# A layer-norm chain laid more densely beside the attention stage, and one weight wait placed later

## The chip, the cores and the metric

The kernel runs on one Trainium2 chip (trn2), on 8 cores at once. Each core works on its own 4,096 of the 32,768 tokens; the cores exchange nothing. The metric is the device time of the slowest core, in microseconds.

## The reference

One "macaron" layer on x of 16 x 2048 tokens with 1024 features, in float32:

```python
x = x + 0.5 * ffn(layernorm(x), gate_w, expert_w)
x = x + attn(layernorm(x), Wq, bq, Wk, bk, Wv, bv, Wo, bo)
x = x + 0.5 * ffn(layernorm(x), gate_w, expert_w)

def attn(x, ...):               # 16 heads of 64 features, no product between tokens
    q = exp(-0.5 * (x @ Wq + bq) ** 2)
    k = exp(-0.5 * (x @ Wk + bk) ** 2)
    v = x @ Wv + bv
    coeff = sum(q * k, over the 64 features of a head)
    return (coeff * v) @ Wo + bo

def ffn(x, gate_w, expert_w):   # 8 experts of 1024 x 1024, the best two weighted by a softmax
    w = softmax(top2(x @ gate_w.T)), put back into 8 columns, 0 elsewhere
    return sum over e of w[:, e] * (x @ expert_w[e].T)
```

The layer norm has no scale or bias. Attention has no product between tokens, so every stage works on a tile of tokens alone.

## The kernel before, in words

Each core holds its tokens as 16 tiles of 256, feature-major: a tile is 8 blocks (c) of 128 features x 256 tokens. The expert weights stay in SBUF in bf16 (16 MB, loaded at the start). The attention weights don't fit beside them. They are cast once into a DRAM copy in bf16 and come back in each attention stage as 16 blocks of 512 KB (four of each matrix, 256 output features each), through four buffers (`Wab`). A block's load is issued by SyncE when the last matmul on the block four places earlier is done (`load_for`, L477).

Tiles go in pairs, eight pairs, a on stream A and b on stream B. A stream owns half of the PSUM banks and its scratch tiles (`SA`, `SC`, `yec`, with the stream's letter behind). For each pair the program has six stages (L677 to L684): experts a, experts b, attention a, attention b, experts a, experts b.

Each engine has one queue of instructions, in the order in which the Python program emits them. `run(heavy, chain, delay, stride)` (L632) sets that order: `heavy` is the generator of a stage, which stops (`yield`) after each group of matmuls; `chain` prepares the other tile's next stage and is advanced by one stop at group `delay` and at each `stride`-th after it. What is left of the chain when the stage ends is emitted at once, without matmuls between.

`attn_phase` (L458) has 25 groups. Groups 1 to 8: for each block of 128 output features (dj) 8 query matmuls into one bank (L504) and 8 key matmuls into another (L514). ACT squares the query bank with its bias (L524) and takes exp (L528), VectorE adds the key bias (L533) and squares (L536), ACT takes exp (L539), VectorE multiplies (L543). Both banks are used again by the next dj. Group 9: 8 matmuls sum over the heads (L553, the coefficient). Groups 10 to 17: value matmuls (L572), one matmul that spreads the coefficient (L587), bias and product on VectorE (L592, L596). Groups 18 to 25: out projection (L612), each evacuated by VectorE, which adds it to x (L622); two banks alternate, so a group waits for the evacuation of the group two before it.

`ln_chain` (L196) has 12 stops: (1) two casts of x to bf16 on VectorE (L211, L214); (2) 8 column-sum matmuls (L224); (3) the first two squares on ACT (L244); (4) to (7) two sum-of-squares matmuls each (L252) and the next square; (8) the statistics, five short operations on VectorE (L267 to L274); (9) Ln, Exp and a copy on ACT (L277 to L281); (10) two broadcast matmuls (L285, L286); (11) two copies on ACT (L289, L291) and the first two of four pairs of normalising operations on VectorE (L299, L302); (12) the other two pairs. Attention b begins when all four are done.

In an expert stage GpSimd scales the tile by the gate's weight for each expert (L426) and TensorE multiplies (L436).

Of the kernel before, what the change touches and what calls it, by code (L numbers as in the profile page):

```python
# [25 lines left out]
def build_program(nt_count=NT):  # L26
# [78 lines left out]
    def op(eng, fn):  # L105
        Q[eng].append(fn)

    def wait(eng, s, val):
        if val and val > 0:
            Q[eng].append(lambda e, _s=sems[s], _v=val: e.wait_ge(_s, _v))  # L110

    def inc(eng, fn, s, by=1):
        C[s] += by
        Q[eng].append(lambda e, _f=fn, _s=sems[s], _b=by: _f(e).then_inc(_s, _b))
        return C[s]

    def drain(eng):
        Q[eng].append(lambda e: e.drain())  # L118

    def wait_tok(eng, tok):  # L120
        if tok:
            wait(eng, tok[0], tok[1])
# [31 lines left out]
    for i in range(16):  # L154
        m, j2 = i // 4, i % 4
# [27 lines left out]
    blk_loaded = {}  # L183
# [274 lines left out]
    def attn_phase(St, t):  # L458
# [6 lines left out]
        def lhs(i, c, dj):  # L465
            buf = i % NWB
            base = buf * 2048 + c * 256 + (dj % 2) * 128
            return Wab[:, base:base + 128]
# [8 lines left out]
        def load_for(idx):  # L477
            if idx >= 16:
                return
            b = order[idx]  # L480
            if idx - NWB >= 0:
                tok = ("pe", blk_free[order[idx - NWB]])
            else:
                tok = attn_pool_free.get(idx % NWB)
            emit_blk_load(t, b, idx, tok)
# [10 lines left out]
        for j2 in range(4):  # L496
            qb, kb = 0 * 4 + j2, 1 * 4 + j2
            wait_tok("pe", blk_loaded[(t, qb)])
            wait_tok("pe", blk_loaded[(t, kb)])
            for dj in (2 * j2, 2 * j2 + 1):  # L500
                if dj >= 1:
                    wait("pe", "se", q_read[dj - 1])
                for c in range(NCH):
                    fn = lambda tt, _c=c, _dj=dj, _i=pos[qb]: tt.matmul(  # L504
                        B0[:, 0:T], lhs(_i, _c, _dj), sa[:, _c * T:(_c + 1) * T],
                        start=(_c == 0), stop=(_c == NCH - 1))
                    if c == NCH - 1:
                        qmm = inc("pe", fn, "pe")
                    else:
                        op("pe", fn)  # L510
                if dj >= 1:
                    wait("pe", "ve", k_read[dj - 1])
                for c in range(NCH):
                    fn = lambda tt, _c=c, _dj=dj, _i=pos[kb]: tt.matmul(  # L514
                        B1[:, 0:T], lhs(_i, _c, _dj), sa[:, _c * T:(_c + 1) * T],
                        start=(_c == 0), stop=(_c == NCH - 1))
                    if c == NCH - 1:
                        kmm = inc("pe", fn, "pe")
                    else:
                        op("pe", fn)  # L520
                wait("se", "pe", qmm)
                if dj >= 1:
                    wait("se", "ve", qk_done[dj - 1])
                q_read[dj] = inc("se", lambda s, _dj=dj: s.activation(  # L524
                    yec[:, 0:T], B0[:, 0:T], ACT.Square,
                    bias=Bias[:, 0 * 8 + _dj:0 * 8 + _dj + 1]), "se")
                drain("se")
                op("se", lambda s: s.activation(yec[:, T:2 * T], yec[:, 0:T], ACT.Exp, scale=-0.5))  # L528
                drain("se")
                wait("ve", "pe", kmm)  # L530
                if dj >= 1:
                    wait("ve", "se", se_prev[dj - 1])
                k_read[dj] = inc("ve", lambda v, _dj=dj: v.tensor_scalar(  # L533
                    yec[:, 2 * T:3 * T], B1[:, 0:T], Bias[:, 1 * 8 + _dj:1 * 8 + _dj + 1], None, ALU.add), "ve")
                drain("ve")
                sq_done = inc("ve", lambda v: v.tensor_mul(  # L536
                    yec[:, 2 * T:3 * T], yec[:, 2 * T:3 * T], yec[:, 2 * T:3 * T]), "ve")
                wait("se", "ve", sq_done)
                se_prev[dj] = inc("se", lambda s: s.activation(  # L539
                    yec[:, 3 * T:4 * T], yec[:, 2 * T:3 * T], ACT.Exp, scale=-0.5), "se")  # L540
                drain("se")
                wait("ve", "se", se_prev[dj])
                qk_done[dj] = inc("ve", lambda v, _dj=dj: v.tensor_mul(  # L543
                    sc[:, _dj * T:(_dj + 1) * T], yec[:, T:2 * T], yec[:, 3 * T:4 * T]), "ve")
                yield
            blk_free[qb] = C["pe"]
            blk_free[kb] = C["pe"]
            load_for(pos[qb] + NWB)
            load_for(pos[kb] + NWB)
# [14 lines left out]
        for dj in range(8):  # L564
            b = 2 * 4 + dj // 2
# [38 lines left out]
        for dj in range(8):  # L604
            b = 3 * 4 + dj // 2
# [26 lines left out]
    def run(heavy, chain, delay=2, stride=1):  # L632
        k = 0
        for _ in heavy:
            k += 1
            if (chain is not None and k >= delay
                    and (k - delay) % stride == 0):
                try:
                    next(chain)
                except StopIteration:  # L640
                    chain = None
        while chain is not None:
            try:
                next(chain)
            except StopIteration:
                chain = None

    def seq(*gens):
        for g in gens:
            for x in g:  # L650
                yield x
# [5 lines left out]
    def store_tile(St, t):  # L657
        buf = t % NXB
        sname = "t%d" % buf
        wait("sy", sname, C[sname])  # L660
        wait("sy", "ve", St.st["ffn_evac"])
        x_stored[t] = (sname, inc("sy", lambda s, _t=t, _b=buf: s.dma_start(
            x_out[_t, :, :, :].rearrange("p c n -> p (c n)"), XT[_b][:, :]), sname, 16))
        St.st["tile_evac"] = St.st["ffn_evac"]
        emit_x_load(t + NXB)
# [8 lines left out]
    for p in range(npair):  # L674
        a, b = 2 * p, 2 * p + 1
        A, Bs = S[0], S[1]
        run(ffn_phase(A, a, first_ffn=(p == 0)), seq(ln_chain(Bs, b, 1), gate_chain(Bs)))  # L677
        run(ffn_phase(Bs, b, first_ffn=(p == 0)), ln_chain(A, a, 2), delay=4, stride=2)
        run(attn_phase(A, a), ln_chain(Bs, b, 2, use_gp=True), delay=6, stride=3)
        run(attn_phase(Bs, b), seq(ln_chain(A, a, 3, use_gp=True), gate_chain(A)), delay=2, stride=1)  # L680
        run(ffn_phase(A, a), seq(ln_chain(Bs, b, 3), gate_chain(Bs)))
        store_tile(A, a)
        nxt = seq(ln_chain(A, 2 * p + 2, 1), gate_chain(A)) if p + 1 < npair else None
        run(ffn_phase(Bs, b), nxt)  # L684
        store_tile(Bs, b)
# [108 lines left out]
```

How the kernel before makes its waits and increments, by code:

```python
    def wait(eng, s, val):  # L108
        if val and val > 0:
            Q[eng].append(lambda e, _s=sems[s], _v=val: e.wait_ge(_s, _v))
# [1 line left out]
    def inc(eng, fn, s, by=1):  # L112
        C[s] += by
        Q[eng].append(lambda e, _f=fn, _s=sems[s], _b=by: _f(e).then_inc(_s, _b))
        return C[s]
```

## Time and profile before

| | us |
|---|---|
| runs | 3118.82, 3124.33, 3166.24 |
| median | 3124.33 |
| profiled execution | 3120.98 |
| its span, slowest core (7) | 3119.4 |
| span of the other cores | 3111.5 to 3118.6 |
| TensorE matmul busy | 2649.2 (85%) |
| GpSimd busy | 1203.7 (39%) |
| VectorE busy | 900.7 (29%) |
| ScalarE (ACT) busy | 526.4 (17%) |

The span runs from the first to the last instruction of the slowest core in one profiled execution; it lies 1.6 us under that execution's device time. Times in the rows below are microseconds from the start of the span. PE is TensorE's matmuls, DVE VectorE, POOL GpSimd, SP SyncE; L12 is line 12 of the kernel. A matmul's time holds its own latency, so in a back-to-back sequence the starts tell the pace.

### The profile page before, as it was taken

What the parts mean: (1) busy time and instruction counts of PE and PEld (TensorE: products, weight loads), DVE (VectorE), ACT (ScalarE), POOL (GpSimd) and SP (SyncE); (2) the same over time, 40 slices, a digit from 0 to 9 for tenths busy, and PEclk for the clock granted to TensorE, in tenths of its full rate; (3) what the DMA queues carried; (4) which work ended last, traced back from release to release, by engine and by line L of the source; (5) the groups of instructions that cost most, each with busy time, mean ns of one, the idle gap of its engine ahead of it and who ended that gap; (6) DMA issues with size and microseconds to landing.
All of it is one profiled execution on the core that took longest, in us unless ns stands there. A gap on an engine that the chain in (4) does not pass through costs nothing.

```text
span 3119.4 us, 58020 instructions; the slowest of 8 cores (3111.5 to 3119.4 us)
## 1 busy us (share of the span) xinstructions
PE 2649.2 (85%) x22240; PEld 2095.9 (67%) x22240; DVE 900.7 (29%) x1920; ACT 526.4 (17%) x1201; POOL 1203.7 (39%) x1059
## 2 busy tenths in 40 slices
PE   0039879997899979997799978999799978999799
PEld 0018648885688747886588846887478855888467
DVE  0012442214422252224332244123522243222430
ACT  0011131103111121111211131111211122111310
POOL 1015215550356305561155503563055611555045
PEclk9999989999999989999899989999899998999999
DMA  9960320104101140203201041011401032010400
GB/s 149 188 163 1 101 89 28 55 1 142 49 28 55 55 135 3 81 2 109 82 28 55 1 149 42 28 55 55 135 15 69 1 109 82 28 42 7 158 27 28
DMA packets 48316, 205.21 MB, mean 66 GB/s; under 512 B 6040, under 2 KB 6040, under 8 KB 42928
## 3 DMA queue, kind: packets, MB, share of 16 engines
q1 hardware_dynamic: 43920, 176.20, 16.5%
q0 software_dynamic: 4128, 25.30, 5.1%
q8 instruction: 185, 3.03, 0.4%
q14 instruction: 83, 0.68, 0.1%
HBM read 201.61 MB, written 25.17 MB: 73 GB/s over the span
## 4 chain that ended last, share of the span: by engine, by line
PE 78%; DMA 7%; DVE 6%; ACT 3%; issue 3%; DVEq 1%; POOL 1%; ACTq 0%; SPq 0%; POOLq 0%
PE P L436 59%; PE P L572 4%; PE P L612 3%; PE P L504 3%; DMA Wexp<-w_exp 3%; PE P L514 2%; DMA Wab<-w_attn 2%; PE P L252 2%; PE P L224 2%; DMA w_attn_bf<-Wab 1%; PE P L320 1%; DVEq L118 1%; PE P L397 1%; DMA Wab<-w_attn_bf 1%; POOL yecA L426 1%
## 5 line engine op out<-in xcount | busy, mean ns | idle before, releaser
L426 POOL TENSOR_TENSOR yecA<-SAA,SCA 128x512 bf16<-128x512 bf16 x512 | 595.5, 1167 | 1369.0 <-ACT SCA L401 959.0
L436 PE MATMUL P<-yecA,Wexp 128*128 128x256 bf16 x8192 | 954.7, 277 | 16.8 <-POOL yecA L426 15.0
L436 PE MATMUL P<-yecB,Wexp 128*128 128x256 bf16 x8192 | 921.1, 273 | 0.0
L436 PEld LDWEIGHTS P<-yecA,Wexp 128*128 128x128 bf16 x8192 | 794.6, 99 | 157.8 <-issue 56.8
L436 PEld LDWEIGHTS P<-yecB,Wexp 128*128 128x128 bf16 x8192 | 790.2, 98 | 118.0 <-issue 27.4
L426 POOL TENSOR_TENSOR yecB<-SAB,SCB 128x512 bf16<-128x512 bf16 x512 | 592.4, 1161 | 373.3 <-PE P L436 367.8
L454 DVE TENSOR_TENSOR XT<-XT,P 128x512 f32<-128x512 f32 x128 | 79.4, 682 | 571.7 <-PE P L436 571.7
L224 PE MATMUL P<-SAA,onescol 128*1 128x256 bf16 x192 | 25.8, 278 | 203.7 <-DVE SAA L211 203.2
L224 PEld LDWEIGHTS P<-SAA,onescol 128*1 128x1 bf16 x192 | 14.5, 84 | 213.2 <-issue 209.3
L504 PE MATMUL P<-SAB,Wab 128*128 128x256 bf16 x512 | 78.5, 304 | 58.3 <-DVE SAB L302 43.0
L244 ACT ACTIVATE yecA<-SAA 128x512 bf16<-128x512 bf16 x96 | 60.4, 629 | 283.9 <-PE P L252 184.4
L299 DVE TENSOR_TENSOR yecA<-SAA,mrbbA 128x512 bf16<-128x512 bf16 x96 | 77.3, 806 | 103.2 <-ACT mrbbA L291 95.3
L244 ACT ACTIVATE yecB<-SAB 128x512 bf16<-128x512 bf16 x96 | 60.4, 629 | 275.6 <-PE P L252 272.5
L504 PEld LDWEIGHTS P<-SAB,Wab 128*128 128x128 bf16 x512 | 51.6, 108 | 81.3 <-issue 70.1
L299 DVE TENSOR_TENSOR yecB<-SAB,mrbbB 128x512 bf16<-128x512 bf16 x96 | 81.2, 846 | 82.0 <-ACT mrbbB L291 75.3
L572 PE MATMUL P<-SAB,Wab 128*128 128x256 bf16 x512 | 82.2, 314 | 25.6 <-DVE SCB L596 25.2
L267 DVE TENSOR_SCALAR MsbA<-P 1x256 f32<-1x256 f32 x24 | 9.8, 409 | 299.7 <-PE P L252 299.7
L267 DVE TENSOR_SCALAR MsbB<-P 1x256 f32<-1x256 f32 x24 | 9.8, 408 | 278.3 <-PE P L252 278.3
L504 PE MATMUL P<-SAA,Wab 128*128 128x256 bf16 x512 | 67.1, 274 | 25.9 <-ACT yecA L524 13.8
L401 ACT CAST SCB<-P 128x256 bf16<-128x256 f32 x128 | 47.7, 373 | 223.1 <-PE P L397 214.7
L622 DVE SCALAR_TENSOR_TENSOR XT<-P,Bias,XT 128x256 f32<-128x256 f32 x128 | 61.9, 484 | 80.1 <-PE P L612 80.1
L572 PEld LDWEIGHTS P<-SAB,Wab 128*128 128x128 bf16 x512 | 51.0, 109 | 48.6 <-issue 36.6
(129 smaller groups left out, 1994.7 us busy)
## 6 DMA issues: line engine op xcount, KB each, us to landing
Wab<-w_attn_bf SPq DMA_DIRECT2D x256, 512.0 KB, 4.2
Wexp<-w_exp POOLq DMA_DIRECT2D x8, 2048.0 KB, 49.2
XT<-x_in SPq DMA_DIRECT2D x16, 1024.0 KB, 5.2
x_out<-XT SPq DMA_DIRECT2D x16, 1024.0 KB, 4.2
Wab<-w_attn POOLq DMA_DIRECT2D x16, 512.0 KB, 11.0
w_attn_bf<-Wab SPq DMA_DIRECT2D x16, 512.0 KB, 8.8
id<-c_id POOLq DMA_DIRECT2D x1, 32.0 KB, 2.3
IND<-c_ind POOLq DMA_DIRECT2D x1, 32.0 KB, 2.2
```

The source lines that it names most:

```text
L224: fn = lambda tt, _c=c: tt.matmul(B3[0:1, 0:T], onescol[:, :], sa[:, _c * T:(_c + 1) * T], start=(_c == 0), stop=(_c == NCH - 1))
L244: sq_done[cp] = inc("se", lambda s, _vv=vv, _p=pp: s.activation(yec[:, _p * 2 * T:(_p + 1) * 2 * T], _vv, ACT.Square), "se")
L252: mm_sq[c] = inc("pe", lambda tt, _c=c, _s=slot: tt.matmul(B3[32:33, 0:T], onescol[:, :], yec[:, _s * T:(_s + 1) * T], start=(_c == 0), st ...
L299: op("ve", lambda v, _s=sv, _y=yv: v.tensor_sub(_y, _s, St.mrbb[:, :].unsqueeze(1).to_broadcast([128, 2, T])))
L426: yd = inc("gp", lambda g, _c=c0, _e=e, _p=pp: g.tensor_mul(yec[:, _p * 2 * T:(_p + 1) * 2 * T].rearrange("p (h n) -> p h n", h=2), sa[:, ...
L436: fn = lambda tt, _e=e, _c=c, _dj=dj, _p=pp, _h=half, _bk=bank, _lo=lo: tt.matmul(_bk[:, _lo:_lo + T], Wexp[:, ((_e * NCH + _c) * D + _dj ...
L454: evac = inc("ve", lambda v, _bk=bank, _xv=xv: v.tensor_tensor(_xv, _xv, _bk[:, :].rearrange("p (h n) -> p h n", h=2), ALU.add), "ve")
L504: fn = lambda tt, _c=c, _dj=dj, _i=pos[qb]: tt.matmul(B0[:, 0:T], lhs(_i, _c, _dj), sa[:, _c * T:(_c + 1) * T], start=(_c == 0), stop=(_c ...
L514: fn = lambda tt, _c=c, _dj=dj, _i=pos[kb]: tt.matmul(B1[:, 0:T], lhs(_i, _c, _dj), sa[:, _c * T:(_c + 1) * T], start=(_c == 0), stop=(_c ...
L572: fn = lambda tt, _c=c, _dj=dj, _i=pos[b], _bk=bank: tt.matmul(_bk[:, 0:T], lhs(_i, _c, _dj), sa[:, _c * T:(_c + 1) * T], start=(_c == 0), ...
L612: fn = lambda tt, _c=c, _dj=dj, _i=pos[b], _bk=bank: tt.matmul(_bk[:, 0:T], lhs(_i, _c, _dj), sc[:, _c * T:(_c + 1) * T], start=(_c == 0), ...
L622: oevac[dj] = inc("ve", lambda v, _dj=dj, _bk=bank: v.scalar_tensor_tensor(xt[:, _dj * T:(_dj + 1) * T], _bk[:, 0:T], Bias[:, 3 * 8 + _dj: ...
```

## The change

Two edits. In `attn_phase` TensorE's wait for the key block of a pair of groups moves from ahead of the first query matmuls to behind them. In the list of stages the layer-norm chain of tile b beside attention a gets delay 4 and stride 2 in place of 6 and 3.

```diff
         for j2 in range(4):
             qb, kb = 0 * 4 + j2, 1 * 4 + j2
             wait_tok("pe", blk_loaded[(t, qb)])
-            wait_tok("pe", blk_loaded[(t, kb)])
             for dj in (2 * j2, 2 * j2 + 1):
                 if dj >= 1:
                     wait("pe", "se", q_read[dj - 1])
@@ -508,6 +507,8 @@
                         qmm = inc("pe", fn, "pe")
                     else:
                         op("pe", fn)
+                if dj == 2 * j2:
+                    wait_tok("pe", blk_loaded[(t, kb)])
                 if dj >= 1:
                     wait("pe", "ve", k_read[dj - 1])
                 for c in range(NCH):
@@ -676,7 +677,7 @@
-        run(attn_phase(A, a), ln_chain(Bs, b, 2, use_gp=True), delay=6, stride=3)
+        run(attn_phase(A, a), ln_chain(Bs, b, 2, use_gp=True), delay=4, stride=2)
```

In the changed kernel L504 is L503, and the lines from L514 on are one higher; the chain's lines keep their numbers.

TensorE's queue before, from the first out-projection group of attention a to the first query matmuls of attention b:

```order
L612 MATMUL P<-SCA,Wab 128x256 x8
L252 MATMUL P<-yecB,onescol 1x256 x2
L612 MATMUL P<-SCA,Wab 128x256 x24
L252 MATMUL P<-yecB,onescol 1x256 x2
L612 MATMUL P<-SCA,Wab 128x256 x24
L252 MATMUL P<-yecB,onescol 1x256 x2
L612 MATMUL P<-SCA,Wab 128x256 x8
L285 MATMUL P<-RbB,onesrow 128x256
L286 MATMUL P<-MRbB,onesrow 128x256
L504 MATMUL P<-SAB,Wab 128x256 x8
```

The same place now, from the last sum-of-squares matmuls on:

```order
L252 MATMUL P<-yecB,onescol 1x256 x2
L573 MATMUL P<-SAA,Wab 128x256 x8
L588 MATMUL P<-CfA,EXPD 128x256
L613 MATMUL P<-SCA,Wab 128x256 x40
L285 MATMUL P<-RbB,onesrow 128x256
L286 MATMUL P<-MRbB,onesrow 128x256
L613 MATMUL P<-SCA,Wab 128x256 x24
L503 MATMUL P<-SAB,Wab 128x256 x8
```

The sum-of-squares matmuls have gone up into the value groups, and the two broadcasts stand behind the fifth out-projection group.

VectorE's queue before, at the end of the same stage:

```order
L622 SCALAR_TENSOR_TENSOR XT<-P,Bias,XT 128x256 x8
L267 TENSOR_SCALAR MsbB<-P 1x256
L268 TENSOR_SCALAR P<-P 1x256
L270 TENSOR_TENSOR MRbB<-MsbB 1x256
L272 TENSOR_TENSOR P<-P,MRbB 1x256
L274 CAST MRbB<-MsbB 1x256
L299 TENSOR_TENSOR yecB<-SAB,mrbbB 128x512
L302 TENSOR_TENSOR SAB<-yecB,rbbB 128x512
```

And now:

```order
L623 SCALAR_TENSOR_TENSOR XT<-P,Bias,XT 128x256
L267 TENSOR_SCALAR MsbB<-P 1x256
L268 TENSOR_SCALAR P<-P 1x256
L270 TENSOR_TENSOR MRbB<-MsbB 1x256
L272 TENSOR_TENSOR P<-P,MRbB 1x256
L274 CAST MRbB<-MsbB 1x256
L623 SCALAR_TENSOR_TENSOR XT<-P,Bias,XT 128x256 x6
L299 TENSOR_TENSOR yecB<-SAB,mrbbB 128x512
L302 TENSOR_TENSOR SAB<-yecB,rbbB 128x512
L299 TENSOR_TENSOR yecB<-SAB,mrbbB 128x512
L302 TENSOR_TENSOR SAB<-yecB,rbbB 128x512
L623 SCALAR_TENSOR_TENSOR XT<-P,Bias,XT 128x256
```

The statistics stand between the first and the second evacuation, and two normalising pairs ahead of the eighth; two more pairs follow it.

## Rows read from the trace of the kernel before

**Rows 1.** The page: the span, and busy time of each engine.
```profile
span 3119.4 us, 58020 instructions; the slowest of 8 cores (3111.5 to 3119.4 us)
...
PE 2649.2 (85%) x22240; PEld 2095.9 (67%) x22240; DVE 900.7 (29%) x1920; ACT 526.4 (17%) x1201; POOL 1203.7 (39%) x1059
```

**Rows 2.** The list of waits: us in total, times, longest us.
```profile
PE P L504 <- DVE SAB L302: 43.0, 8, 5.4
...
PE P L285 <- ACT RbB L281: 31.1, 8, 3.9
...
PE P L504 <- DMA Wab<-w_attn_bf: 9.3, 7, 2.2
```

**Rows 3.** Timeline of TensorE, end of attention a: start us, us, instruction [idle before].
```profile
2191.32 1.03 PE L612 MATMUL P<-SCA,Wab 128*128 128x256 bf16 x8 [1.38 <-DVE SCA L596]
2192.29 0.38 PE L252 MATMUL P<-yecB,onescol 128*1 128x256 bf16 x2
2192.60 2.83 PE L612 MATMUL P<-SCA,Wab 128*128 128x256 bf16 x24
...
2198.73 1.05 PE L612 MATMUL P<-SCA,Wab 128*128 128x256 bf16 x8
2203.66 0.26 PE L285 MATMUL P<-RbB,onesrow 1*128 1x256 bf16 x1 [3.88 <-ACT RbB L281]
...
2209.45 1.86 PE L504 MATMUL P<-SAB,Wab 128*128 128x256 bf16 x8 [5.42 <-DVE SAB L302]
```

**Rows 4.** Timeline of VectorE, the same stretch.
```profile
2192.48 0.48 DVE L622 SCALAR_TENSOR_TENSOR XT<-P,Bias,XT 128x256 f32<-128x256 f32 x1 [1.40 <-PE P L612]
...
2199.88 0.48 DVE L622 SCALAR_TENSOR_TENSOR XT<-P,Bias,XT 128x256 f32<-128x256 f32 x1 [0.81 <-PE P L612]
2200.28 0.40 DVE L267 TENSOR_SCALAR MsbB<-P 1x256 f32<-1x256 f32 x1
...
2202.22 0.28 DVE L274 CAST MRbB<-MsbB 1x256 bf16<-1x256 f32 x1
2205.03 0.42 DVE L299 TENSOR_TENSOR yecB<-SAB,mrbbB 128x512 bf16<-128x512 bf16 x1 [2.53 <-ACT mrbbB L291]
...
2208.58 0.42 DVE L302 TENSOR_TENSOR SAB<-yecB,rbbB 128x512 bf16<-128x512 bf16 x1
```

**Rows 5.** Timeline of ACT, the same stretch.
```profile
2204.56 0.37 ACT L291 CAST mrbbB<-P 128x256 bf16<-128x256 f32 x1
```

**Rows 6.** Timeline of TensorE, from the query/key to the value groups.
```profile
2173.11 1.03 PE L514 MATMUL P<-SAA,Wab 128*128 128x256 bf16 x8 [1.04 <-DVE yecA L533]
2176.39 1.03 PE L553 MATMUL P<-SCA,IND 128*16 128x256 bf16 x8 [2.25 <-DVE SCA L543]
2177.26 1.67 PE L224 MATMUL P<-SAB,onescol 128*1 128x256 bf16 x8
2178.87 1.89 PE L572 MATMUL P<-SAA,Wab 128*128 128x256 bf16 x8
```

**Rows 7.** Timeline of VectorE, query/key groups.
```profile
2166.55 0.48 DVE L533 TENSOR_SCALAR yecA<-P,Bias 128x256 bf16<-128x256 f32 x1 [0.80 <-PE P L514]
...
2170.42 0.69 DVE L211 CAST SAB<-XT 128x1024 bf16<-128x1024 f32 x1
2171.55 0.69 DVE L214 CAST SAB<-XT 128x1024 bf16<-128x1024 f32 x1 [0.44 <-issue]
```

**Rows 8.** Line L191, the two weight loads issued from 1432.3 to 1432.8.
```profile
DMA to landing us min/median/max: 3.8/5.0/6.1
```

**Rows 9.** Timeline of TensorE, the group that uses them.
```profile
1439.11 1.03 PE L504 MATMUL P<-SAA,Wab 128*128 128x256 bf16 x8 [2.22 <-DMA Wab<-w_attn_bf]
```

**Rows 10.** Windows: stretch, length, busy by engine (instructions), granted clock, DMA, GB/s.
```profile
2177.20:2180.70 3.50, 3.50 (x20) 1.87 (x17) 0.41 (x1) 0.13 (x1) 0.00 (x0) 0.54 0.44 166
...
2209.50:2214.80 5.30, 5.30 (x26) 3.65 (x27) 0.96 (x3) 1.31 (x3) 0.00 (x0) 0.50 0.00 0
...
1484.10:1487.70 3.60, 3.60 (x18) 2.56 (x19) 0.00 (x0) 0.89 (x2) 0.00 (x0) 0.50 0.00 0
```

## The prediction

> **What bounds the kernel now.** I read the page's busy shares first: TensorE is busy 85% of a span of 3119.4 us, no other engine more than 39% [rows 1]. So what counts is idle time of TensorE, and the list of waits by engine and line says where it lies. Three of its rows concern the lines of this change [rows 2]. At the start of the attention stage of tile b, TensorE waits 43.0 us in 8 waits for the last normalisation operation (L302 of stream B), one wait a pair of tiles, and a step earlier 31.1 us in 8 waits for the ACT chain that ends at L281. The third, for loads of the attention weights, is 9.3 us in 7 waits. One pair in the order of time shows the first two as one hole [rows 3]: the last out-projection matmul of tile a ends at 2199.78 (2198.73 + 1.05), two short broadcast matmuls stand at 2203.66, and stream B's first query matmul starts at 2209.45. That is 9.67 us with 0.4 us of work in it. In the hole VectorE and ACT do, one after the other, what is left of stream B's layer norm: statistics 2200.28 to 2202.50, then Ln, Exp and a copy, the broadcasts on TensorE, copies of them to 2204.93, four pairs of normalising operations 2205.03 to 2209.00 [rows 4, 5]. It is a chain of short dependent steps and nothing else is ready for TensorE.
>
> **How the sum is set up.** Stream B's chain has 12 stops, and after the last group of stage a whatever is left of it is emitted at once. With delay 6 and stride 3 the 25 groups of the stage take 7 stops, and 5 remain; with delay 4 and stride 2 they take 11 and one remains (normalising pairs 3 and 4). I walk through one pair, with its durations, against the profiled execution of 3120.98 us; the middle one of the runs is 3124.33, 3.4 us more, so the sum can be set against either. There are 8 such stages.
>
> **Out-projection and hole.** Let t0 be the start of the first out-projection group (2191.32). Before, t0 to B's start is 18.13 us [rows 3]. After:
> - Groups without the sums of squares between them take 0.92 us each (24 matmuls in 2.83 us, of which some 0.1 is the last one's own end). The first result is evacuated from t0+1.16 to t0+1.64 (2192.48, 0.48 long [rows 4]).
> - The statistics now stand directly behind it on VectorE. They end 2.14 us after an evacuation ends (2200.36 to 2202.50), so at t0+3.78; only then comes the second evacuation, to t0+4.34. The fourth group needs that bank and could start at t0+2.76. It starts at t0+4.48: a new stall of 1.7 us.
> - Groups 4 and 5 end at t0+6.3, the broadcasts (their inputs ready since about t0+4.7, the ACT steps take 1.4 us, from 2202.22 to 2203.66 [rows 3, 4]) take 0.3, groups 6 and 7 end at t0+8.45, group 8 at t0+9.4.
> - VectorE evacuates group 7 to t0+9.2, then does pairs 1 and 2: four operations, half of the eight from 2205.03 to 2209.00, 2.0 us [rows 4]; then evacuation 8 to 11.8, then pairs 3 and 4 to 13.8. With 0.45 us from the last of them to the matmul (2209.00 to 2209.45) stream B starts at t0+14.3.
>
> That is 18.1 - 14.3 = 3.8 us saved in a stage. The hole shrinks from 9.7 to 4.9 us, and 1.7 comes back as the stall at the fourth group. If that stall were absent the saving would be 5.5; if the statistics also delayed the third evacuation, some 3.
>
> **Value stage.** Four pairs of sum-of-squares matmuls now stand in it, where one did: 3 x 0.31 us (2192.29 to 2192.60 [rows 3]) = +0.9. ACT, which makes the squares, has nothing else to do there. The 8 column sums of L224 leave the place before the first value group, where they take 1.61 us at the low clock of that moment (2177.26 to 2178.87 [rows 6]) and about 0.9 at the full one. If value matmuls stand at the low clock in their place, which I assume, the gain is 0.9. These two cancel: bounds -0.7 and +0.9 a stage, taken 0.
>
> **Query/key stage.** The two casts hold VectorE from 2170.42 to 2172.24, between a product and the next key bias. They now stand after group 4 instead of group 6 [rows 7]. In place of 2166.55 the key bias of group 5 starts at about 2167.9, and its key-side bank is read 1.35 us later. Walking the loop on with its own durations (bias 0.48, product 0.29, an ACT step 0.42 to 0.47) the second half of group 6 stands 1.2 us late, group 7 too, group 8 only 0.1, since it waited before for exactly these casts. The column sums, now between groups 6 and 7, fall into the time in which group 7 waits for ACT: they cost nothing. The coefficient matmul at 2176.39 [rows 6] comes 0.2 us earlier. Bounds: 1.35 late (nothing is made good) and 1.0 early (the whole wait before 2173.11 goes). I take 0.2 early.
>
> **The key block's wait.** Of two loads issued 0.45 us apart the first lands after 3.8 us and the second after 6.1 [rows 8], so the query block is there some 1.9 us before the key block; TensorE started only after 2.22 us of idle [rows 9]. Without the key's wait a query group of 0.9 us can run in that time. A group also waits about 0.7 us without any load, for ACT. So of the 9.3 us [rows 2], 7 x 0.7 stay; 4.4 can go. In stage a the casts now lie over the same time, which hides the load's lateness too, and loads that arrive just late without being named add a little. I take 5 us in all, from 0 to 12 (9.3 and as much again of unnamed ones, halved).
>
> The row says that the query block lands first. The Trainium skill, page "DMA: Bandwidth & Descriptors", section "Queues, rings and completion order", says that completion is not first-in first-out even for one issuing engine, so a later load's semaphore may be full earlier. Were that so here, the edit would be worth 0 and the sum 5 us smaller; by the landing times the trace goes the other way, and I keep the 5.
>
> **Clock.** After the hole the matmuls run at 1.2 GHz: in this pair for 5.3 us (granted clock 0.50), in another for 3.6 [rows 10]. They lose half of that, 2.65 and 1.8 us. A wait of 2.25 us before the coefficient matmul was also followed by a low stretch, of 3.5 us with 0.54 [rows 6, 10]. So I expect the hole of 4.9 us to be followed by a low stretch as after the short wait, 3.5 us instead of about 4.7: 0.6 us a stage, bounds 2.65 (no low stretch) and -1.7 (one more of 3.4 us, behind the new stall).
>
> **Sum.** Per stage 3.8 + 0 + 0.2 + 0.6 = 4.6; times 8 is 37; plus 5 is 42. 3120.98 - 42 = 3079 us, 0.985 of the middle run. The rest of the pair (four expert stages and stream B's attention) keeps its order of instructions; it moves earlier as a whole. B's first loads start at the ends of out-projection groups and need 4 to 6 us; B's third and fourth blocks are used two groups later, so the shorter hole still covers them.
>
> **Rivals.**
> - *The clock stays up.* The hole is half as long, and if stream B starts at the full clock in all stages the gain is 2.65 - 0.6 = 2 us more, and up to 1.7 more where the low stretch before the value groups goes too. For it: 5 us of idle are removed. Against: a low stretch also followed 2.25 us of waiting. 8 x 2 + 6 = 22 more: 3057. The Trainium skill, page "TensorE: Matmul & The Clock Gate", Part 1, says that the throttled clock is the default and activity releases it; by that, less idle time can only help this rival. The trace agrees in that the low stretches stand only behind waits.
> - *The hole only moves.* The stall at the fourth out-projection group is longer (statistics, then two evacuations in arrears), and the casts in the query/key stage cost their 1.35 us. 3.0 - 1.35 = 1.65 a stage, 13 + 5 = 18: 3103.
> - *Slower.* The stall of 1.7 us stands 2.8 us behind one of 1.4 us in front of the first group [rows 3]. If this is enough to drop the clock, the five last groups run at 1.2 GHz, 5 x 0.9 = 4.6 us more, and since the hole follows, the clock does not come back before B's third group (2.65 us as before plus 0.9). With 1.35 for the casts: 3.8 - 4.6 - 0.9 - 1.35 = -3.1 a stage, +24, -5 for the loads: 3140. It decides once over two thirds of that low stretch appears. Against: between the two waits stand 2.8 us of matmuls at the full clock, and the value stage ahead of them has none of such waits.
> - *Not what it says.* The key block's wait is moved but never the last one: 0 in place of 5 us, 3084; inside the forecast.
>
> **How the numbers follow.** Forecast 0.62 (own range 3062 to 3095), clock stays up 0.17, hole only moves 0.16, slower 0.05. A change of 2%, 62 us, is about what a measurement of this kernel can tell from none: faster than that means below 3062. The first rival lies mostly there, and a tail of the forecast: 0.19. Slower by 2% needs 3187, beyond even the slow rival's value: 0.02. Within 2%: 0.79. The range runs to 3052, for most of the first rival, and to 3106, for the third case: 3052 to 3106.
>
> **What would show it.** TensorE's wait for L302 of stream B at 4.5 to 5.5 us in 8 waits, hardly changed in size since the chain's other waits go; the 31.1 us wait at L285 gone; a new wait of some 14 us in 8 at the out-projection for the evacuation of its line; statistics between the first and second evacuation; two normalising pairs before the eighth; waits for the weight loads under 5 us. I am wrong if the hole still is over 7 us, if the granted clock falls inside the out-projection, or if the expert stages change their length.

## The result, and the profile after

The changed kernel takes 3073.84 us (median of 9 runs); the ratio to the kernel before is 0.984, 95% interval 0.983 to 0.985. Some runs of both kernels were disturbed on one die and are left out of the ratio. The forecast was 3079, in a range of 3052 to 3106, and "within 2%": the gain is 47 to 50 us where 42 were forecast. The profiled execution's span is 3072.3 us on its slowest core; the mean over the eight cores fell from 3115.8 to 3067.0, 48.8 us.

The page, span and busy time by engine. Against [rows 1], TensorE has 3.8 us less busy time in a span 47.1 us shorter: what went is idle time, and the little that went of the busy time is matmuls that ran at 1.2 GHz before.

```profile
span 3072.3 us, 58020 instructions; the slowest of 8 cores (3062.1 to 3072.3 us)
...
PE 2645.4 (86%) x22240; PEld 2092.5 (68%) x22240; DVE 898.4 (29%) x1920; ACT 527.5 (17%) x1201; POOL 1203.6 (39%) x1059
```

The list of waits (us in total, times, longest us). L503 was L504, the other attention lines are one higher.

```profile
PE P L503 <- DVE SAB L302: 34.3, 8, 4.3
...
PE P L554 <- DVE SCA L544: 17.6, 8, 2.3
...
PE P L613 <- DVE XT L623: 13.0, 8, 1.6
...
PE P L515 <- DVE yecA L534: 9.2, 16, 0.7
```

Against [rows 2]: the wait for stream B's last normalising operation is 34.3 us in 8 in place of 43.0, and no wait of L285 for L281 of stream B is left (31.1). Together the hole before attention b is 4.3 us in place of 9.7. The second row, the coefficient matmul's wait of 2.2 us a pair, is as in [rows 6]. New is the third, 1.6 us eight times at the out-projection, for its own evacuation. The fourth is the query/key loop's wait for VectorE, where the casts now make themselves felt: at most 0.7 us, in place of the 1.04 of [rows 6]. Of the query and key matmuls' waits for weight loads none is left on this core (9.3 on the core of [rows 2]); the mean of the same rows over the eight cores is 11.6 us before and 0.5 after.

The timeline of TensorE in the sixth pair, the one of [rows 3, 6] (this time on core 5):

```profile
2147.15 1.54 PE L554 MATMUL P<-SCA,IND 128*16 128x256 bf16 x8 [2.19 <-DVE SCA L544]
2148.62 1.89 PE L573 MATMUL P<-SAA,Wab 128*128 128x256 bf16 x8
...
2161.81 2.81 PE L613 MATMUL P<-SCA,Wab 128*128 128x256 bf16 x24 [1.34 <-DVE SCA L597]
2166.24 1.91 PE L613 MATMUL P<-SCA,Wab 128*128 128x256 bf16 x16 [1.62 <-DVE XT L623]
...
2168.40 2.82 PE L613 MATMUL P<-SCA,Wab 128*128 128x256 bf16 x24
2175.51 1.86 PE L503 MATMUL P<-SAB,Wab 128*128 128x256 bf16 x8 [4.29 <-DVE SAB L302]
```

The three groups from 2161.81, the stall of 1.62, two groups, the two broadcasts (2168.08 and 2168.20, not shown), three groups, then the hole. From the first out-projection group to stream B's first is 13.70 us; before 18.13. The timeline of VectorE for the same stretch shows who sets it:

```profile
2162.97 0.48 DVE L623 SCALAR_TENSOR_TENSOR XT<-P,Bias,XT 128x256 f32<-128x256 f32 x1 [1.40 <-PE P L613]
...
2165.30 0.28 DVE L274 CAST MRbB<-MsbB 1x256 bf16<-1x256 f32 x1
2165.62 0.88 DVE L623 SCALAR_TENSOR_TENSOR XT<-P,Bias,XT 128x256 f32<-128x256 f32 x2
...
2170.43 0.48 DVE L623 SCALAR_TENSOR_TENSOR XT<-P,Bias,XT 128x256 f32<-128x256 f32 x1 [0.39 <-PE P L613]
2170.83 0.41 DVE L299 TENSOR_TENSOR yecB<-SAB,mrbbB 128x512 bf16<-128x512 bf16 x1
...
2172.93 0.48 DVE L623 SCALAR_TENSOR_TENSOR XT<-P,Bias,XT 128x256 f32<-128x256 f32 x1 [0.16 <-issue]
...
2174.83 0.43 DVE L302 TENSOR_TENSOR SAB<-yecB,rbbB 128x512 bf16<-128x512 bf16 x1
```

The first evacuation is at 2162.97. The statistics (the last of them at 2165.30) hold the second one until 2165.62, where two stand back to back: this is the stall. The seventh evacuation is at 2170.43, behind it pairs 1 and 2 (2170.83 to 2172.77), the eighth evacuation, pairs 3 and 4, which end at 2175.25, and stream B starts 0.26 us later. The hole is filled by VectorE, end to end.

The clock in windows (stretch, length, busy by engine, granted clock, DMA share, GB/s): behind the coefficient's wait it is low as before, through the out-projection it is full in spite of the stall, behind the hole it is low again, for 2.7 us of matmuls in place of the 5.3 or 3.6 of [rows 10].

```profile
2147.50:2150.90 3.40, 3.40 (x17) 1.68 (x15) 0.41 (x1) 0.59 (x1) 0.00 (x0) 0.50 0.47 189
2161.80:2171.20 9.40, 7.77 (x66) 5.97 (x66) 5.46 (x13) 1.80 (x5) 0.00 (x0) 1.00 0.56 168
...
2175.50:2178.20 2.70, 2.69 (x13) 1.88 (x14) 0.00 (x0) 0.65 (x2) 0.00 (x0) 0.50 0.00 2
```

Where the time went, from the first and the last matmul of each part in the timelines of all eight cores, as the mean over cores and the 8 pairs, in us. "Rest" is from the end of attention b to the next attention a; "low" is the time in which matmuls ran at a granted clock of 0.5 in the parts named.

| per pair | q/k a | value a | out a | hole | q/k b | value b | out b | rest | mean span |
|---|---|---|---|---|---|---|---|---|---|
| before | 22.20 | 14.76 | 8.45 | 9.68 | 24.89 | 20.83 | 9.01 | 252.04 | 3115.8 |
| after | 21.48 | 14.34 | 9.41 | 4.29 | 24.38 | 20.96 | 9.01 | 251.69 | 3067.0 |
| low before | 0.4 | 3.0 | 0 | | 5.1 | 6.9 | 0 | 4.9 | |
| low after | 0.1 | 2.7 | 0 | | 4.0 | 7.3 | 0 | 4.2 | |

The sum of the differences is 6.3 us a pair, of which 4.4 in the out-projection and the hole. Times eight it is 50; the part ahead of the first attention stage was 1.4 us longer.

### The profile page after: what moved, and what is told of

It is laid out like the page before. It is cut to its first block, busy times and chain, and to the rows that moved or that the text cites. A ratio compares the mean times of both kernels' runs of the same rounds, so it can differ in the third digit from the quotient of the medians.

```text
span 3072.3 us, 58020 instructions; the slowest of 8 cores (3062.1 to 3072.3 us)
## 1 busy us (share of the span) xinstructions
PE 2645.4 (86%) x22240; PEld 2092.5 (68%) x22240; DVE 898.4 (29%) x1920; ACT 527.5 (17%) x1201; POOL 1203.6 (39%) x1059
## 4 chain that ended last, share of the span: by engine, by line
PE 79%; DVE 6%; DMA 6%; issue 3%; ACT 3%; DVEq 2%; POOL 1%; ACTq 0%; SPq 0%; POOLq 0%
PE P L436 60%; PE P L573 4%; PE P L503 3%; PE P L613 3%; DMA Wexp<-w_exp 3%; PE P L515 2%; DMA Wab<-w_attn 2%; PE P L252 2%; PE P L224 1%; DVEq L118 1%; DMA w_attn_bf<-Wab 1%; PE P L320 1%; PE P L397 1%; POOL yecA L426 1%; PE P L588 1%
## 5 line engine op out<-in xcount | busy, mean ns | idle before, releaser
L224 PEld LDWEIGHTS P<-SAA,onescol 128*1 128x1 bf16 x192 | 14.5, 84 | 212.7 <-issue 208.8
L503 PE MATMUL P<-SAB,Wab 128*128 128x256 bf16 x512 | 75.7, 297 | 50.9 <-DVE SAB L302 34.3
L503 PEld LDWEIGHTS P<-SAB,Wab 128*128 128x128 bf16 x512 | 50.2, 105 | 71.9 <-issue 62.5
L613 PE MATMUL P<-SCA,Wab 128*128 128x256 bf16 x512 | 60.3, 272 | 23.8 <-DVE XT L623 13.0
```

The source lines that it names most:

```text
L224: fn = lambda tt, _c=c: tt.matmul(B3[0:1, 0:T], onescol[:, :], sa[:, _c * T:(_c + 1) * T], start=(_c == 0), stop=(_c == NCH - 1))
L503: fn = lambda tt, _c=c, _dj=dj, _i=pos[qb]: tt.matmul(B0[:, 0:T], lhs(_i, _c, _dj), sa[:, _c * T:(_c + 1) * T], start=(_c == 0), stop=(_c ...
L613: fn = lambda tt, _c=c, _dj=dj, _i=pos[b], _bk=bank: tt.matmul(_bk[:, 0:T], lhs(_i, _c, _dj), sc[:, _c * T:(_c + 1) * T], start=(_c == 0), ...
```

## The experiments

All are variants of the two kernels, and each ratio is to the kernel before, run on the same chip. A gain "by the ratios" is the difference of two ratios times 3124 us; the 95% interval of each ratio is 3 to 8 us to either side. The same table for all of them stands behind the last one, with the mean span of the profiled execution as a second measure. My theory was the prediction's: the hole is VectorE's work behind the last group; what is moved forward costs where it falls into a full queue; late loads are covered; the clock falls behind TensorE's waits. Rivals are in the expectations.

**Each edit alone.** First only the moved wait:

```diff
-        run(attn_phase(A, a), ln_chain(Bs, b, 2, use_gp=True), delay=4, stride=2)
+        run(attn_phase(A, a), ln_chain(Bs, b, 2, use_gp=True), delay=6, stride=3)
```

> Only the key block's wait is moved; the chain stays at delay 6, stride 3. Theory (as in the prediction: the query block lands about 2 us before the key block and its matmuls fill that time): 3 to 7 us faster than before, ratio 0.998 to 0.999; TensorE's waits for the weight loads under half of the 9.3 us; the hole before attention b stays at 9.7 us. Rival (the time gained is waited for at the next group, since the loop through ACT and VectorE sets the pace): ratio 1.000 within 0.0005, with the load waits turned into waits for ACT or VectorE.

Measured: 3121.66 us, ratio 0.9985 (0.9975 to 0.9995). Its waits:

```profile
PE P L503 <- DVE SAB L302: 41.9, 8, 5.3
...
PE P L515 <- DMA Wab<-w_attn_bf: 0.8, 1, 0.8
```

The loads' waits fall from 9.3 to 0.8 us (mean of the cores: 11.6 to 1.0), the query/key stage of a from 22.20 to 21.79, and the waits of the same matmuls for ACT and VectorE rise by 5.4 (mean of the cores: 38.0 to 43.3). So about half of the 10.6 us is waited for again at the next groups, as the rival had it for all of it, and the prediction for 0.7 us of each wait. The run is 0.15% faster: 5 us, inside what was expected; the interval lies under 1 (2 to 8 us). In its profiled execution the mean span is that of before: the 3.3 us gained in eight query/key stages of a are taken back by small amounts in the other parts (the value stage of a, the query/key stage of b and the rest are each 0.15 to 0.18 us a pair longer, the start 1.1 us in all). The clock was low for 0.3 to 0.5 us a pair more in each of these three parts; that does not come from the edit by anything the trace shows.

Then only the denser chain:

```diff
-        run(attn_phase(A, a), ln_chain(Bs, b, 2, use_gp=True), delay=6, stride=3)
+        run(attn_phase(A, a), ln_chain(Bs, b, 2, use_gp=True), delay=4, stride=2)
```

> Only the chain is laid at delay 4, stride 2; the key block's wait stays where it was. Theory (the hole of 9.7 us shrinks to 4.3, 1.6 us come back at the fourth out-projection group, and the casts after group 4 cover late loads even without the moved wait): 42 to 48 us faster than before, ratio 0.985 to 0.9865, and the query/key stage of a under 21.8 us on average. Rival (the missing load waits in the changed kernel are the moved wait's work): 38 to 42 us faster, with load waits of 7 us or more in the attention stages.

Measured: 3079.69 us, ratio 0.9855 (0.9828 to 0.9882).

```profile
PE P L504 <- DVE SAB L302: 35.2, 8, 4.4
...
PE P L504 <- DMA Wab<-w_attn_bf: 14.5, 10, 2.6
```

The hole and the stall are those of the full change. The query/key stage of a takes 21.59 us, as the theory said, so the casts do cover late loads there. But load waits are left, as the rival said: 14.5 us in 10 on this core, the worst of the eight, 4.9 in the mean (11.6 before, 0.5 with both edits). Both were half right, and the times of the two versions can't be told apart (the intervals of 0.9855 and 0.9841 overlap; the mean spans differ by 2.3 us). By the ratios the moved wait is worth 5 us alone and 4 on top of the chain, by the mean spans 0 and 2: an estimate of 0 to 5 us of the 49, and only the run of the wait alone is clear of its noise.

**The stall at the fourth group.** The out-projection over four banks, from the changed kernel:

```diff
-            bank = B0 if dj % 2 == 0 else B1
+            bank = St.B[dj % 4]
             if dj % 2 == 0:
                 wait_tok("pe", blk_loaded[(t, b)])
-            if dj >= 2:
-                wait("pe", "ve", oevac[dj - 2])
+            if dj >= 4:
+                wait("pe", "ve", oevac[dj - 4])
```

> The changed kernel with the out-projection over four PSUM banks in place of two, in both attention stages. Theory (the stall at the fourth group comes from the statistics in VectorE's queue; TensorE then runs ahead, but stream B can't start before VectorE is through): the 13.0 us wait for the evacuation is gone, the out-projection of a takes 7.8 us in place of 9.4, the hole grows from 4.3 to about 4.7 us, so that 1.2 us a stage remain, 10 us in all: 3064. Rival (the whole stall is recovered, as nothing else is bound there): 13 us faster, 3061, hole unchanged at 4.3. Second rival (VectorE is the bound through the whole stretch): same time, the hole grows by 1.6 us.

Measured: 3065.00 us, ratio 0.9804 (0.9788 to 0.9819), 11 us under the changed kernel by the ratios. TensorE and VectorE in the sixth pair, core 1:

```profile
2155.19 4.53 PE L613 MATMUL P<-SCA,Wab 128*128 128x256 bf16 x40 [1.35 <-DVE SCA L597]
2160.12 0.26 PE L285 MATMUL P<-RbB,onesrow 1*128 1x256 bf16 x1 [0.40 <-DVE XT L623]
...
2160.42 2.79 PE L613 MATMUL P<-SCA,Wab 128*128 128x256 bf16 x24
2167.53 1.86 PE L503 MATMUL P<-SAB,Wab 128*128 128x256 bf16 x8 [4.31 <-DVE SAB L302]
```

```profile
2158.68 0.28 DVE L274 CAST MRbB<-MsbB 1x256 bf16<-1x256 f32 x1
2158.99 1.66 DVE L623 SCALAR_TENSOR_TENSOR XT<-P,Bias,XT 128x256 f32<-128x256 f32 x4
...
2161.57 0.48 DVE L623 SCALAR_TENSOR_TENSOR XT<-P,Bias,XT 128x256 f32<-128x256 f32 x1 [0.92 <-PE P L613]
```

Five groups run through; 0.40 us are left of the wait of 1.6. VectorE makes up its arrears with four evacuations in 1.66 us (2158.99) and is level again before the sixth, for which it waits 0.92 us. So the hole stays at 4.3, and 1.3 us a stage are gained in the out-projection. Over the whole pair less is left in this execution: its mean span is 7.3 us shorter, not 11, with the query/key stage of b and the rest 0.3 and 0.4 us longer and 0.7 and 0.9 us more of them at the low clock. The statistics' place is the cause of the stall, and the first rival describes the rest better than my theory, which had VectorE in arrears to the end of the stage.

**Fewer and more stops inside the stage.** Delay 6 with stride 2 (ten stops inside):

> The changed kernel with delay 6, stride 2: ten stops inside the stage, so the ACT copies and all four normalising pairs are left for its end, and the casts stand after group 6 as before the change. Theory (the hole is VectorE's work behind the last group, 2 us for two pairs, each queued operation counting): the hole is 5.2 us in place of 4.3, the query/key stage of a 21.8 in place of 21.5, the column sums hidden again in front of the coefficient matmul, the statistics' stall of 1.6 us one place later: about 10 us slower than the changed kernel, 3084. Rival (what counts is the number of stops left, not VectorE's work): the hole doubles for two stops in place of one, to 8 us, 3105.

Measured: 3072.12 us, ratio 0.982 (0.980 to 0.984): not slower than the changed kernel, where I expected 10 us. The hole is 4.77 us (expected 5.2, rival 8), the query/key stage of a 21.84 as expected. The stall of 1.6 us now stands in front of the sixth group, two groups later, as the statistics now stand behind the third evacuation. What I had missed is the value stage, 12.94 us in place of 14.34:

```profile
2145.49 1.03 PE L224 MATMUL P<-SAB,onescol 128*1 128x256 bf16 x8
2147.82 1.03 PE L554 MATMUL P<-SCA,IND 128*16 128x256 bf16 x8 [1.29 <-DVE SCA L544]
2148.78 1.05 PE L573 MATMUL P<-SAA,Wab 128*128 128x256 bf16 x8
...
2167.35 1.91 PE L613 MATMUL P<-SCA,Wab 128*128 128x256 bf16 x16 [1.61 <-DVE XT L623]
...
2175.28 1.87 PE L503 MATMUL P<-SAB,Wab 128*128 128x256 bf16 x8 [4.72 <-DVE SAB L302]
```

```profile
2147.50:2151.00 3.50, 3.18 (x26) 2.20 (x26) 1.35 (x4) 1.17 (x2) 0.00 (x0) 1.00 0.82 300
```

The column sums now stand in front of the coefficient matmul, TensorE waits 1.29 us there in place of 2.2, and the clock stays at 1.00 behind it: no matmul of the value stage of a ran at 1.2 GHz on any core. Compare 2148.78 here (8 matmuls in 1.05 us) with 2148.62 after the change (1.89). Two things differ in front of the coefficient, 8 more matmuls and 0.9 us less of waiting; this run doesn't say which of them keeps the clock up.

Delay 2 with stride 2 (all twelve inside):

> The changed kernel with delay 2, stride 2: all 12 stops inside the stage, nothing is left for its end. Theory: the hole shrinks from 4.3 to about 1.8 us, but the statistics now stand in VectorE's queue in front of the last value group's evacuation, and the first out-projection group waits 2 us longer for it; the squares on ACT fall into the query/key loop and lengthen it by up to 1 us; together 0 to 1 us a stage better, and the clock after the short hole stays up at least in part (up to 2 us a stage): 3050 to 3074, middle 3064. Rival (VectorE's and ACT's loops are full in the query/key and value stages, so each chain step moved there costs its whole length): 10 us or more slower than the changed kernel.

Measured: 3081.38 us, ratio 0.9855 (0.983 to 0.988). That is above what I expected, and by the ratios 4 us above the changed kernel, on the rival's side but short of its 10; the intervals overlap.

```profile
2168.16 5.28 PE L613 MATMUL P<-SCA,Wab 128*128 128x256 bf16 x24 [3.48 <-DVE SCA L597]
...
2178.95 1.03 PE L613 MATMUL P<-SCA,Wab 128*128 128x256 bf16 x8 [1.46 <-DVE XT L623]
2181.39 1.86 PE L503 MATMUL P<-SAB,Wab 128*128 128x256 bf16 x8 [1.41 <-DVE SAB L302]
```

```profile
2166.80:2173.60 6.80, 5.43 (x26) 3.50 (x26) 2.02 (x6) 0.87 (x3) 0.00 (x0) 0.50 0.25 92
...
2180.40:2187.20 6.80, 5.81 (x28) 4.05 (x29) 2.12 (x6) 1.57 (x4) 0.00 (x0) 0.50 0.26 85
```

The hole is as small as expected, 1.35 us. But the statistics delay the last value product, TensorE waits 3.48 us in front of the first out-projection group, and behind this wait the first groups run at 1.2 GHz: 24 matmuls in 5.28 us instead of 2.8. The out-projection of a takes 11.41 us in place of 9.41 (4.6 us of it at the low clock), the query/key stage 22.60 in place of 21.48. In this pair the clock falls again at the start of b, though the wait there is 1.4 us only (with 1.46 a group earlier); so it does in 44 of the 64 pairs of the eight cores. And in front of the coefficient of a TensorE waits 1.79 us here, with two sum-of-squares matmuls ahead: the value stage holds low clock in 1 pair of 64, where it did in 50 behind the 2.2 us of the change. This is the low clock inside the out-projection of the prediction's slower rival; it comes with a wait of 3.5 us in front of the stage, not with one of 1.6.

**The clock behind the hole.** 36 matmuls without use in the hole (their result is never read):

```diff
+        for _ in range(36):
+            op("pe", lambda tt: tt.matmul(P[6][:, 0:T], Wexp[:, 0:128], Wexp[:, 0:T], start=True, stop=True))
         run(attn_phase(Bs, b), seq(
```

> The changed kernel with 36 matmuls on constant operands, written to an unused PSUM bank, in TensorE's queue between the last out-projection group of a and the first query group of b (3.9 us of work in a hole of 4.3; their result is never read). Theory (the first groups of b run at 1.2 GHz for 4.0 us a stage because TensorE idles before them, at a price of half of that): the granted clock is 1.00 through the start of b, the query/key stage of b 2 us shorter, 16 us in all: 3058. Rival (the low stretch there is not due to this hole, or the loop of ACT and VectorE hides it): no change within 3 us. Second rival (the extra matmuls delay the first query group): up to 5 us slower.

Measured: 3060.14 us, ratio 0.9787 (0.9772 to 0.9801), 17 us under the changed kernel by the ratios, 12 by the mean spans. The sixth pair on core 2, timeline and windows:

```profile
2161.80 4.09 PE L682 MATMUL P<-Wexp 128*128 128x256 bf16 x36
2166.26 1.03 PE L503 MATMUL P<-SAB,Wab 128*128 128x256 bf16 x8 [0.36 <-DVE SAB L302]
```

```profile
2162.00:2166.20 4.20, 3.90 (x36) 3.23 (x34) 3.37 (x8) 0.00 (x0) 0.00 (x0) 1.00 0.72 239
2166.20:2170.00 3.80, 3.68 (x32) 2.91 (x32) 1.02 (x3) 1.31 (x3) 0.00 (x0) 1.00 0.00 0
```

Granted clock 1.00 before and after b's start; 8 matmuls in 1.03 us where [rows 3] have 1.86. The query/key stage of b is 22.56 us in place of 24.38, 1.8 less: a little under half of the 4.0 at the low clock. The hole itself is 4.29, as after the change. Neither rival came.

The same, with 16 more in front of both coefficient matmuls:

```diff
+        for _ in range(16):
+            op("pe", lambda tt: tt.matmul(St.B[2][:, 0:T], Wexp[:, 0:128], Wexp[:, 0:T], start=True, stop=True))
         wait("pe", "ve", qk_done[7])
```

> The kernel with 36 extra matmuls in the hole before b, and 16 more (1.7 us, result never read) in front of the coefficient matmuls of both attention stages, where TensorE waits 2.2 and 1.8 us. Theory (the low clock in the value stage follows this wait): the value stage of a, which holds 2.6 us of matmuls at 1.2 GHz, is 1.3 us shorter, that of b 0.5 to 1.5 shorter, so 12 to 20 us less than with the 36 alone: 3044. Rival (a wait of 2 us is too short to cause it, other idle time in the query/key stage does): no change within 3 us. Second rival (16 matmuls delay the coefficient): up to 5 us slower.

Measured: 3051.44 us, ratio 0.976 (0.974 to 0.978), 8 us better than with the 36 alone by the ratios, 11 by the mean spans, where I expected 12 to 20.

```profile
PE P L556 <- DVE SCA L544: 3.5, 8, 0.4
```

```profile
2135.00:2140.00 5.00, 5.00 (x39) 3.13 (x37) 3.64 (x8) 0.63 (x1) 0.00 (x0) 1.00 0.49 150
...
2189.00:2201.00 12.00, 8.79 (x39) 4.34 (x36) 6.36 (x15) 0.36 (x1) 0.00 (x0) 0.58 0.26 88
```

The wait in front of the coefficient of a is 0.4 us a stage, its value stage is 13.15 us in place of 14.30 and holds nothing at the low clock. In b nothing is gained: its value stage still holds 7.4 us at the low clock (the second window), which stands behind other waits, for products that VectorE delivers late because tile a's normalising operations stand before them in its queue (first TensorE, then VectorE shortly before the first of these waits ends):

```profile
2191.55 1.87 PE L575 MATMUL P<-SAB,Wab 128*128 128x256 bf16 x8 [2.08 <-DVE SCB L599]
...
2194.80 1.86 PE L575 MATMUL P<-SAB,Wab 128*128 128x256 bf16 x8 [1.06 <-DVE SCB L599]
```

```profile
2189.76 0.43 DVE L302 TENSOR_TENSOR SAA<-yecA,rbbA 128x512 bf16<-128x512 bf16 x1
...
2190.42 0.48 DVE L595 TENSOR_SCALAR yecB<-P,Bias 128x256 bf16<-128x256 f32 x1 [0.23 <-issue]
```

**Together.** Four banks and both groups of extra matmuls, run twice:

> Four banks in the out-projection together with both groups of extra matmuls. Theory (the parts are independent: the stall at the fourth group, the clock behind the hole, the clock behind the coefficient's wait): the gains add, 3044 less 11: 3033, ratio 0.970. Rival (they share the same idle time): less than 5 us better than the extra matmuls alone.

> The same kernel as the run of four banks with both extras, again with more rounds, for its interval: 3038 to 3042, ratio 0.971 to 0.974, and clearly under the changed kernel's 0.984.

Measured: ratios 0.9724 (0.9695 to 0.9752) and 0.9727 (0.9711 to 0.9742), fastest run 3037.86 us. The gains add, to within 6 us of the forecast 3033: this is the fastest version, 1.2% under the changed kernel. And with delay 6, which puts the column sums where the 16 stood:

> Delay 6, stride 2 with four banks in the out-projection and the 36 extra matmuls before b, none in front of the coefficient matmul. Theory from the pieces measured so far (mean of the cores, us a stage: query/key of a 21.8, value 12.9, out-projection 8.3, hole 4.8, query/key of b 22.6; value of b and the rest as in the run of both extras): 0.9 us a stage more than four banks with both extras, so 3040 to 3050. It says that the column sums in front of the coefficient matmul keep the clock up as well as 16 extra matmuls do: no low clock in the value stage of a. Rival (the low stretch comes back once the hole's timing is changed): 2 to 3 us of low clock there, 3055 or more.

Measured: 3046.34 us, ratio 0.974 (0.9725 to 0.976), as expected from the pieces; the value stage of a takes 12.95 us, with no low clock.

| per pair, us | q/k a | value a | out a | hole | q/k b | value b | rest | mean span | ratio |
|---|---|---|---|---|---|---|---|---|---|
| before | 22.20 | 14.76 | 8.45 | 9.68 | 24.89 | 20.83 | 252.04 | 3115.8 | 1 |
| wait moved alone | 21.79 | 14.91 | 8.45 | 9.53 | 25.06 | 20.76 | 252.22 | 3115.8 | 0.9985 |
| chain alone | 21.59 | 14.32 | 9.41 | 4.39 | 24.60 | 21.10 | 251.72 | 3069.4 | 0.9855 |
| the change | 21.48 | 14.34 | 9.41 | 4.29 | 24.38 | 20.96 | 251.69 | 3067.0 | 0.9841 |
| four banks | 21.56 | 14.41 | 8.08 | 4.32 | 24.65 | 20.66 | 252.12 | 3059.7 | 0.9804 |
| delay 6, stride 2 | 21.84 | 12.94 | 9.79 | 4.77 | 24.39 | 20.96 | 251.70 | 3064.7 | 0.9822 |
| delay 2, stride 2 | 22.60 | 15.10 | 11.41 | 1.35 | 24.01 | 20.90 | 251.77 | 3070.1 | 0.9855 |
| 36 extra | 21.44 | 14.30 | 9.44 | 4.29 | 22.56 | 21.10 | 251.99 | 3055.4 | 0.9787 |
| 36 and 16 extra | 21.44 | 13.15 | 9.41 | 4.30 | 22.56 | 21.30 | 251.64 | 3044.1 | 0.9762 |
| the same, four banks | 21.47 | 13.17 | 8.06 | 4.32 | 22.55 | 20.94 | 252.13 | 3035.3 | 0.9724 |
| delay 6, stride 2, banks, 36 | 21.78 | 12.95 | 8.43 | 4.73 | 22.56 | 21.07 | 251.62 | 3039.1 | 0.9743 |

The two measures differ by up to some 5 us for a single step: by the mean spans, four banks give 7 us, the 36 matmuls 12, the 16 more 11, and all three 32, where the ratios give 11, 17, 8 and 36. The order of the versions is the same by both but for delay 2, stride 2 and the chain alone, which have one ratio.

## Why the prediction was right

Each step can be set beside a row of the table.

- *Out-projection and hole.* Forecast 3.8 us a stage, measured 4.4 (18.13 to 13.70). The stall came where it was put, 1.62 us against 1.7. The hole was sized 4.9 and is 4.29: VectorE's walk was taken 0.35 us too long in all (to t0+13.8, measured t0+13.44), and stream B's start follows its last operation by 0.26 us, not by the 0.45 of [rows 3, 4]. The timeline shows the stall to be the statistics' doing, and so do the four-bank run, where most of it goes, and delay 6, where it moves with them to the sixth group; the runs with other delays show that the hole goes with what VectorE has left.
- *Query/key stage and the key block's wait.* Forecast 0.2 us a stage and 5 us in all, 0.8 a pair if all of it falls into a; measured 0.72 in a. The casts displaced the next key bias by less than I took, as they now follow each other at once: 1.80 us from the end of the product to the bias, below, where it was 2.16 before (2170.32 to 2172.48), with a gap of 0.44 between the casts [rows 7]. How much of the 0.72 comes from this and how much from the loads is not separated: the wait alone gave 0.41, the chain alone 0.61. The column sums cost nothing there, as forecast: the next query matmuls follow them without a wait. One reading was wrong without effect: the key block of [rows 8] lands 2.8 us behind the query block, not 1.9, since the 0.45 us between the two issues adds to the 2.3 and was taken off. Over all pairs of such loads before the change it is 1.0 to 3.3 us, 1.5 in the mean, and never the other way round; the sum used only the 0.9 us of one query group. That half of the load waits would stay as waits for ACT was right in size. The rival "not what it says" did not come: alone, the wait gave 2 to 8 us.

```profile
2136.48 0.29 DVE L544 TENSOR_TENSOR SCA<-yecA 128x256 bf16<-128x256 bf16 x1 [0.61 <-ACT yecA L540]
2136.86 0.69 DVE L211 CAST SAB<-XT 128x1024 bf16<-128x1024 f32 x1
2137.64 0.69 DVE L214 CAST SAB<-XT 128x1024 bf16<-128x1024 f32 x1
2138.57 0.48 DVE L534 TENSOR_SCALAR yecA<-P,Bias 128x256 bf16<-128x256 f32 x1 [0.23 <-PE P L503]
```

- *Value stage.* Forecast 0, measured 0.42 less. The two parts did not quite cancel, and 0.3 us less of it ran at the low clock. The assumption behind it (the clock falls behind the coefficient's wait as before) held, but it was a choice of the schedule and no constant: with delay 6 and stride 2 the same matmuls stand in front of the coefficient and the clock stays up, 1.4 us a stage. I had not priced where in a wait a filler stands. That the forecast of 0 lies so near is in part the luck of two cancelling terms that were not measured one by one.
- *Clock behind the hole.* Forecast 0.6 us a stage, measured 0.51 in the query/key stage of b, from 5.1 us at the low clock to 4.0.
- *The rest of the pair* was taken as unchanged and is 0.35 us a pair shorter, all of it clock (4.9 to 4.2 us at 1.2 GHz, half of the difference); value b is 0.13 longer. That is 2 us less in eight pairs and was not in the sum. By the sign that the prediction set for itself, expert stages of another length, this is 0.14% of the 252 us, with the order of instructions unchanged.

So the sum was 42 where 47 to 50 came: 5 us from the hole's size, 3 from the value stage, 2 from the rest, and the other way 1 from the start and 1 to 2 from the query/key stages and their clock. The other signs came: no wait at L285 for L281 of stream B is left, the new wait is 13.0 us in 8 ("some 14"), the waits for loads are under 5; the wait for L302, 4.3 us, lies just under the 4.5 to 5.5 that were named. The rival "clock stays up" did not come: a hole of 4.3 us still pulls the clock down, in all 64 pairs; it was priced at 2 us a stage more, and the extra matmuls show 1.8. "The hole only moves" did not come either: the casts were made good. Of the slower rival, the mechanism exists and was seen at delay 2, at under half its size (2.0 us more in the out-projection, 4.6 in the rival), but not at the waits of this change.

What stays open: why the profiled execution with the wait alone had more low clock than the one before, and how much of its 0.15% is the moved wait's own. The moved wait was not tried in stream b alone.

## What to carry to other kernels

An interleaved chain should be judged by what is left of it when the stage ends, and by the queue into which each of its steps falls: the statistics, 2.1 us on VectorE, cost 1.6 us between two evacuations with two banks, 0.3 with four, and more than their length where they delayed the first input of a stage (2.1 us more of waiting, and the clock); the casts, moved to another place of the query/key stage, cost nothing that shows. Where a hole can't be closed, what follows it can run at the low clock: of the 4.3 us a stage that the later versions took off these parts, 3.0 came from matmuls without use in the waits. Moving matmuls that had to be done into the wait in front of the coefficient did as well for the value stage behind it, though the hole grew by 0.4 us with that schedule. Walk one period, queue by queue, and keep each part's length: the sums of parts met the combined versions to within 0.3% of the time, which is 5 to 8 us here.

## What was not expected of the hardware

- TensorE's granted clock depended on waits of 1 to 2 us: behind a wait of 2.2 us in front of the coefficient of a the value groups ran at 0.50 for about 3.4 us in 54 of 64 pairs before and 50 after; behind one of 1.8 us (delay 2) in 1 of 64, behind one of 1.3 us with 8 one-column matmuls ahead of it (delay 6) in none. Behind 4.3 us of idle filled with 3.9 us of matmuls whose result is not used, the clock stayed at 1.00 in all pairs on all cores.
- The length of the wait alone does not decide it. The coefficient of b waits 1.8 us in all the versions without matmuls put there, and a low stretch began in it or within 2 us behind it in 17 of 64 pairs before, in 40 with the wait moved alone, in 9 after the change and in 1 with four banks. At the out-projection's first group of a, behind a wait of 1.35 to 1.4 us, one began in 3 of 64 pairs with four banks and in 3 with the 36 extra matmuls, in none before and after.
- In the pair shown of delay 2 a wait of 1.4 us was followed by a low stretch where another of 1.46 us stood 2.4 us ahead of it; 1.6 us alone, inside the out-projection, did not in any pair after the change.
- VectorE left 0.44 us between the two casts of stream B where they stood behind group 6 (in all 64 stages of each of the four kernels with that place) and 0.09 where they stood behind group 2 or 4; the rows name no releaser for the gap.
